# Scan stage of a six-layer kernel: parts of B and C made by ScalarE and TensorE, front products in two PSUM banks, decays in two

## What is computed

```
x_and_res = inputs @ W_in
x, res = jnp.split(x_and_res, 2, axis=-1)            # 256 channels each
x = jax.nn.silu(_depthwise_conv_same(x, K_conv, b_conv))   # 4 taps
x_dbl = inputs @ W_x                                  # 64 + 16 + 16 columns
delta, Bm, Cm = jnp.split(x_dbl, [DT_RANK, DT_RANK + D_STATE], axis=-1)
delta = jax.nn.softplus(delta @ W_dt + b_dt)
# for each channel and each of 16 states, over the 512 tokens:
#   h = exp(delta * A) * h + delta * x * Bm ;  y += h * Cm
y = y + x * D
y = y * jax.nn.silu(res)
return y @ W_out + b_out
```

## Time and profile before

| | us |
|---|---|
| median of three runs | 1669.47 (1667.58 to 1669.6) |
| the profiled execution, its own time | 1665.65 |
| its span | 1663.5 |
| first scan of the stage starts (in the span) | 787.7 |
| last scan of the stage starts | 1290.2 |
| busy over the whole span: TensorE, VectorE, GpSimd, ScalarE | 1404.0, 1172.5, 533.9, 513.2 |

### The profile page before, as it was taken

How to read it: one execution, slowest core, us unless ns; L and a number is a source line. 1 busy time by engine, 2 the same in 40 slices (tenths; PEclk the granted TensorE clock), 3 DMA queues, 4 the chain that set the end, 5 groups by cost and what they waited for, 6 DMA issues and landing times.

```text
span 1663.5 us, 21345 instructions
## 1 busy us (share of the span) xinstructions
PE 1404.0 (84%) x7226; PEld 1033.1 (62%) x7226; DVE 1172.5 (70%) x2629; ACT 513.2 (31%) x999; POOL 533.9 (32%) x447
## 2 busy tenths in 40 slices
PE   2887886595999999976888878878878599999998
PEld 2884545595899999952333333333323489999996
DVE  3786763585577776532998899999999557777753
ACT  2203444200222222223545445455353022222221
POOL 1150000001000000002788788888899100000000
PEclk9998997797899999986998989989998799999998
DMA  5550000553333333301332222323222233333330
GB/s 154 205 185 1 1 0 1 203 206 102 103 103 103 103 103 103 102 1 46 84 101 79 78 91 78 98 70 93 93 96 73 98 108 109 109 109 109 109 109 13
DMA packets 93162, 155.11 MB, mean 93 GB/s; under 512 B 11703, under 2 KB 21374, under 8 KB 92926
## 3 DMA queue, kind: packets, MB, share of 16 engines
q1 hardware_dynamic: 93054, 153.76, 28.5%
HBM read 150.31 MB, written 3.41 MB: 92 GB/s over the span
## 4 chain that ended last, share of the span: by engine, by line
PE 68%; DVE 16%; issue 8%; POOL 3%; ACT 2%; DMA 2%; DVEq 0%; POOLq 0%; SPq 0%; ACTq 0%
PE bank L1080 21%; PE bank L1198 7%; PE bank L1083 7%; PE bank L942 5%; PE bank L1142 3%; PE bank L973 2%; PE bank L1040 2%; DVE xe L1557 2%; DVE hs L1557 2%; DVE both L1549 2%; PE bank L1025 2%; POOL both L598 2%; PE bank L1092 2%; PE bank L1022 2%; PE bank L982 2%
## 5 line engine op out<-in xcount | busy, mean ns | idle before, releaser
L1080 PE MATMUL bank<-wqkv_sb,xe 128*128 128x192 f32 x2048 | 370.5, 334 | 10.0 <-DVE xe L1493 9.8
L1080 PEld LDWEIGHTS bank<-wqkv_sb,xe 128*128 128x128 f32 x2048 | 340.1, 194 | 21.4 <-DVE xe L1493 15.0
L1198 PE MATMUL bank<-both,ident 128*128 128x512 f32 x512 | 267.4, 650 | 17.3 <-DVE both L1549 16.4
L566 POOL TENSOR_TENSOR rstd<-ve,half_neg 128x4 f32<-128x4 f32 x32 | 37.6, 1173 | 734.0 <-DVE ve L1251 734.0
L843 ACT ACTIVATE bank<-dt,A 128x512 f32<-128x512 f32 x256 | 172.7, 685 | 169.6 <-DVE xe L1557 92.8
L1198 PEld LDWEIGHTS bank<-both,ident 128*128 128x128 f32 x512 | 105.0, 212 | 151.2 <-issue 108.3
L598 POOL TENSOR_TENSOR both<-du,prob 128x512 f32<-128x512 f32 x128 | 161.1, 1271 | 36.0 <-DVE xe L1557 19.8
L598 POOL TENSOR_TENSOR both<-du,prT 128x512 f32<-128x512 f32 x128 | 160.8, 1271 | 17.0 <-DVE hs L1557 12.5
L1557 DVE TENSOR_TENSOR_SCAN hs<-bank,both 128x512 f32<-128x512 f32 x128 | 153.7, 1212 | 0.0
L1557 DVE TENSOR_TENSOR_SCAN xe<-bank,both 128x512 f32<-128x512 f32 x128 | 152.8, 1210 | 0.3 <-issue 0.3
L942 PE MATMUL bank<-exp_sb,xe 128*128 128x128 f32 x1024 | 128.1, 283 | 27.1 <-DVE xe L1376 26.5
(11 more groups left out here) (261 smaller groups left out, 2011.4 us busy)
## 6 DMA issues: line engine op xcount, KB each, us to landing
dt<-w_rows SPq DMA_DIRECT2D x128, 256.0 KB, 4.2
du<-w_rows SPq DMA_DIRECT2D x128, 256.0 KB, 5.2
prob<-bc_dram SPq DMA_DIRECT2D x64, 256.0 KB, 3.3
prT<-bc_dram SPq DMA_DIRECT2D x64, 256.0 KB, 3.3
dt<-g_dram SPq DMA_DIRECT2D x32, 256.0 KB, 5.6
du<-g_dram SPq DMA_DIRECT2D x32, 256.0 KB, 6.7
g<-g_dram SPq DMA_DIRECT2D x32, 256.0 KB, 6.5
u<-g_dram SPq DMA_DIRECT2D x32, 256.0 KB, 6.4
```

The lines of the kernel that those rows point to most:

```text
L566: pool.tensor_tensor(rstd[:], ve[:], half_neg[:, 0:NT], ALU.pow).then_inc(ln_rstd, 1)
L1080: m = pe.matmul(bank[4 + j // 2][:, (j % 2) * 3 * HD:(j % 2 + 1) * 3 * HD], x_e, wqkv_sb[:, e, :], start=(e == 0 and j % 2 == 0), stop=(e ...
L1198: pe.matmul(bank[4 + k % NH][:], ident[:], hc[k % HRING], start=False, stop=(SUM_RANK[k] == sums_of(k // UNITS, k % NH))).then_inc(hc_used, 1)
```

## The change

It does six things in the scan stage.

- **Parts of B and C.** The steps `rows` and `bcT`, VectorE's copy and the five split operations go. ScalarE copies B and C from the dlt product twice, once as bf16 (the first part, into `bcT3`) and once as float32 (`bc_rows`, there before too). TensorE then makes, in float32, bc_rows minus the parts so far (one product with the identity, one with `less`, which holds -1), and ScalarE copies the result as the next bf16 part; this happens twice.
- **Banks.** Front products lie in two banks: conv0, conv1, z0, res0 in bank 2; xT, dlt and the two rests, z1, res1, out in bank 7. Each waits for the one before it in its own bank.
- **Decays.** Bank 2 was one of three decay banks, so two remain. ScalarE now makes the decay of scan U+1 in slot U, and it waits for the scan two before.
- **Slots.** All tables of front steps are new; `out` moves from slot 6 to 7, the addition to x from 8 to 10, the DMA of B and C to DRAM from slot 2 to slot 31.
- **Order within a front.** dlt stands between the two halves of conv0.
- **Waits.** th, lz and thr each have one buffer, and ScalarE now waits for VectorE's use of them, as bank 7 no longer orders it.

```
-FRONT7 = {"xT": -8, "rows": -6, "conv0": -4, "dlt": 0, "bcT": 2, "conv1": 8, "z0": 12, "z1": 16, "res0": 20, "res1": 22}
-OUT7 = 6
+FRONT7 = {"xT": -7, "dlt": -4, "conv0": -3, "conv1": 5, "z0": 11, "z1": 12, "res0": 17, "res1": 20}
+OUT7 = 7
+FRONT_IN = {"xT": 7, "dlt": 7, "conv0": 2, "conv1": 2, "z0": 2, "z1": 7, "res0": 2, "res1": 7, "out": 7}
...
-        decay = [bank[0], bank[6], bank[2]]
+        decay = [bank[0], bank[6]]
+        front_bank = {name: bank[i] for name, i in FRONT_IN.items()}
...
+                    if b >= 2:
+                        act.wait_ge(C_ps, seen(states_on_dve(NS * (b - 1))))
+                    act.activation(bcT3[par][0:32, :], front_bank["dlt"][DR:W3, :], ACT.Copy).then_inc(bcT_sb, 1)
+                    act.activation(dlt[0:DR, :], front_bank["dlt"][0:DR, :], ACT.Copy).then_inc(dlt_sb, 1)
                     if b:
                         act.wait_ge(bc_out, 16 * b)
-                    act.activation(bc_rows, bank[7][DR:W3, :], ACT.Copy).then_inc(dlt_sb, 1)
-                    yield
-                    act.wait_ge(bank7_ps, seen(IN7["bcT", b]))
-                    act.activation(bcT3[par][:], bank[7][0:W3, 0:L // 2].bitcast(BF16), ACT.Copy).then_inc(bcT_sb, 1)
-                    yield
+                    act.activation(bc_rows, front_bank["dlt"][DR:W3, :], ACT.Copy).then_inc(dlt_sb, 1)
+                    yield
+                    tanh_u(0)
+                    yield
+                    for part in (1, 2):
+                        act.wait_ge(part_ps, seen(2 * b + part))
+                        act.activation(bcT3[par][32 * part:32 * (part + 1), :], front_bank["dlt"][0:32, :], ACT.Copy).then_inc(bcT_sb, 1)
+                        yield
...
-                steps = on_clock(front, (-10, -7, -1, 1, 3, 11, 13, 14, 17, 18, 21, 23))
+                steps = on_clock(front, (-10, -6, -3, -1, 1, 3, 7, 12, 13, 15, 16, 18, 22))
                 for U in SCAN_CLOCK:
-                    if 0 <= U + 2 < ALL:
-                        decay_of(U + 2)
+                    if 0 <= U + 1 < ALL:
+                        decay_of(U + 1)
                     due(steps, U)
...
+                    for part in range(2):
+                        pe.wait_ge(dlt_sb, seen(2 * (b + 1)))
+                        pe.wait_ge(bcT_sb, seen(3 * b + part + 1))
+                        pe.matmul(front_bank["dlt"][0:32, :], ident[0:32, 0:32], bc_rows, start=True, stop=False)
+                        m = pe.matmul(front_bank["dlt"][0:32, :], less[0:32 * (part + 1), :], bcT3[par][0:32 * (part + 1), :], start=False, stop=True)
+                        m.then_inc(part_ps, 1)
+                        yield
...
-                steps = on_clock(front, (-8, -6, -4, -2, 0, 2, 8, 10, 12, 16, 20, 22), back, (OUT7,))
+                steps = on_clock(front, (-7, -5, -4, -3, -1, 2, 3, 5, 11, 12, 17, 20), back, (OUT7,))
...
-                steps = on_clock(front, (-13, -11, -5, 0, 12, 15, 19, 22, 24), back, (4, 5, 8))
+                steps = on_clock(front, (-13, -11, 1, 9, 15, 18, 20, 24), back, (4, 5, 10))
```

More of the change, by code:

```diff
@@ L160 @@
                + [(UNITS * (b + 1) + OUT7, "out", b) for b in range(NB)])
-BEFORE7 = {TURNS[i + 1][1:]: TURNS[i][1:] for i in range(len(TURNS) - 1)}
+BEFORE7 = {}
+for i in (2, 7):
+    there = [turn[1:] for turn in TURNS if FRONT_IN[turn[1]] == i]
+    BEFORE7.update(zip(there[1:], there))
 IN7 = {turn[1:]: i + 1 for i, turn in enumerate(t for t in TURNS if t[1] not in ("xT", "out"))}
@@ L1132, in front @@
                     pe.wait_ge(xT_sb, seen(g + 1))
[L1133 to L1137, removed]
                     def conv(h):
                         into_bank7(f"conv{h}", b)
-                        pe.matmul(bank[7][:], bias3[:, P + h * P:P + (h + 1) * P], ones3[:], start=True, stop=False)
+                        to = front_bank[f"conv{h}"][:]
+                        pe.matmul(to, bias3[:, P + h * P:P + (h + 1) * P], ones3[:], start=True, stop=False)
                         for tap in range(4):
-                            m = pe.matmul(bank[7][:], wcv[:, tap, h * P:(h + 1) * P], xpad[:, tap:tap + L], start=False, stop=(tap == 3))
+                            m = pe.matmul(to, wcv[:, tap, h * P:(h + 1) * P], xpad[:, tap:tap + L], start=False, stop=(tap == 3))
                             if tap == 1:
@@ L1146, in conv @@
                         yield
-                    yield from conv(0)
+                    conv0 = conv(0)
+                    pe.wait_ge(xT_sb, seen(g + 1))
+                    next(conv0)
+                    yield
                     into_bank7("dlt", b)
-                    pe.matmul(bank[7][0:W3, :], wx_sb[:], xpad[:, 1:L + 1], start=True, stop=True).then_inc(bank7_ps, 1)
+                    pe.matmul(front_bank["dlt"][0:W3, :], wx_sb[:], xpad[:, 1:L + 1], start=True, stop=True).then_inc(bank7_ps, 1)
                     yield
[L1152 to L1157, removed]
-                    yield
+                    next(conv0)
+                    yield
+                    for part in range(2):
[5 more added lines that the diff above has]
+                        yield
                     yield from conv(1)
@@ L1161, in front @@
                         into_bank7(f"z{h}", b)
-                        pe.matmul(bank[7][:], wdt_sb[:, h * P:(h + 1) * P], dlt[:], start=True, stop=True).then_inc(bank7_ps, 1)
+                        pe.matmul(front_bank[f"z{h}"][:], wdt_sb[:, h * P:(h + 1) * P], dlt[:], start=True, stop=True).then_inc(bank7_ps, 1)
                         yield
@@ L1170, in back @@
                     into_bank7("out", b)
-                    pe.matmul(bank[7][:], ones3[:, 0:P], bout3[:], start=True, stop=False)
+                    pe.matmul(front_bank["out"][:], ones3[:, 0:P], bout3[:], start=True, stop=False)
                     for h in range(NH):
@@ L1539, in back @@
                     dve.wait_ge(acc_ps, seen(NB + b + 1))
-                    dve.tensor_tensor(seq(b), seq(b), bank[7][:], ALU.add).then_inc(acc_used, 1)
+                    dve.tensor_tensor(seq(b), seq(b), front_bank["out"][:], ALU.add).then_inc(acc_used, 1)
                     yield
```

64 lines of the change are left out of this document (27 added, 37 removed).

## The result

The changed kernel takes 1652.71 us (median of six runs, 1648.43 to 1655.66) against 1668.82 for the kernel before; the ratio is 0.9904, with a 95% interval from 0.9886 to 0.9922. It is 16 us faster. The forecast was 1629: right in its direction, and 24 us too good.

A forecast was written before the change was run, and what follows sets the result against it. VectorE's queue was taken as the bound. From 1665.65 us profiled, 30.7 in the scans (53.3 removed less 22.6 new stalls) and 9.7 in the lead-in gave 1625.2, so a 1629 median; range 1614 to 1640 (0.55).

The forecast's parts named there:

- VectorE's work: Scan stage: VectorE's work after the change is 57.2 us a cycle, the floor, above GpSimd's 55.4.
- The waits that go: VectorE's waits in the scans: 14.7 for tanh, 6.5 "issue", 4.1 for C, 3.3 for the output product disappear.
- The split: Removed split operations and copy on VectorE, third scan to last: 24.7 us saved, 4.1 a cycle.
- Lead-in: Before the first scans, the front chain gets shorter: scan 2 comes 9.7 us earlier, bounds 6 to 12.
- Slot 12: ScalarE's table load and az waiting for z0 make scan 14 2.4 us late, first element 1.2; 15.6 in all.
- Slot 9: Product waits for its C row on TensorE: 0.4 us, seven times, 2.8 in all.
- Slot 29, the three copies: Three ScalarE copies and dlt's arrival each make scan 31 0.35 us late; 0.7, six times, 4.2.
- Rival 1: TensorE's clock falls to half around slot 25, costing 3.0 to 4.3 us six times: 1647 to 1655; chance 0.20.
- Rival 3: Slower: with two decays, ScalarE's waits for TensorE stop scans; 10 us more a cycle gives 1689; chance 0.05.
- Rival 2: No new stalls in the scans: cycle falls to its floor, up to 22.6 us less, 1606; chance 0.12.
- Rival 4: GpSimd becomes the bound: two microseconds lost at its du steps, cycle 63, time 1643; chance 0.04.
- Rival 5: No change: removed time returns as waits for the same tiles at other slots, 1668 to 1673; chance 0.04.

The follow-up runs named there:

- the fillers: Changed kernel plus four half-width float32 products on TensorE in slots 24, 25 and 26, results overwritten unread; 1642.39 us, ratio 0.9842.
- third buffer: Changed kernel with three buffers in place of two for the parts of C (`bcT3`); 1636.68 us, ratio 0.9813.
- version with all edits: Changed kernel plus third buffer, the fillers, table load alone in slot 10, softplus from slot 14, dlt in slot 27, two copies in slot 28; 1612.94 us.

## Why the prediction was right and wrong

- **VectorE's work, 57.2 a cycle: right in size, in part by luck.** It is busy 57.28 in the changed kernel, and cycles are 57.9 once no scan waits for a decay. But the prediction took off 4.1 for the split, the mean of the cycles, where the cycle that it started from had 4.7, and the norm grew by 0.9: 60.98 less 4.7 plus 0.9 is 57.2.
- **The waits that go, 28.6 by four rows: nearly right.** In the stretch of scans 3.2 for a product are left, one in the first element and one in the last. A wait of 1.6 for the output product stands behind the last scan and doesn't count.
- **The split, 24.7: over-sized by about 5.** The operations are gone, but between scan 2 and the last scan VectorE's busy time fell by 19.7, from 461.1 to 441.4. Two operations of the norm, on 128x4 elements, take 4.5 longer in all (below, on VectorE and GpSimd), though the change left them as they were, and so did the prediction. In the kernel before, taking away four of five operations gave 12.2 in place of 18.7, because two of the casts left stood for 3.3 each.
- **Lead-in, 9.7: right,** 11.1.
- **Slot 12, 15.6: right in kind and nearly in size.** 1.10 + 6 x 1.95 = 12.8; az did wait for z0 (six times 0.86), a little less than the 1.35 counted.
- **Slot 9, 2.8: right.** It was 0.40, six times (2.4).
- **Slot 29, the three copies, 4.2: this step failed.** It measured 28.3. The prediction let the copies start when dlt lands. They also wait for the last row of C of the running element, a wait that the diff shows, and I priced it at nothing. And it took TensorE to be at full clock here. At full clock the lateness is 1.06 for copies and dlt (0.7 was counted) and 2.0 for the C row; that makes 3.06, measured once and reproduced by the fillers. The half clock adds 1.6 to 2.3 in each of the other five. The third buffer and the fillers show the two causes, each alone and both together.
- **Rival 1, the clock: it happened,** with 0.20 given to it, and at half its price, some 2 in place of 3.0 to 4.3 a cycle (with the third buffer, one cycle lost 3.2 by it). That the measured 1652.71 lies in its range of 1647 to 1655 is luck: about half of the loss is the C row, which this rival does not have. The fillers gave back 10 us with two buffers (1652.71 to 1642.39) and 5 with three (1636.68 to 1631.26).
- **Rival 3: its mechanism, at half its size.** It said that every wait of ScalarE for TensorE stops the scans, and asked for 6.7 more in each cycle than counted. The copies of slot 29 are such a wait, and the three stalls cost 3.5 more a cycle than counted (43.5 less 22.6, over six).
- **Rivals 2, 4 and 5 did not occur.** Rival 2's time, 1606, is nearly reached by the version with all edits, which took the stalls away one by one.

The sum: 53.3 less 22.6 was forecast for the stretch of scans. With the stalls as measured it is 53.3 less 43.5 (12.8, 2.4 and 28.3), or 9.8. The 3.2 of waits that did not go and the 4.5 of the norm take that to 2.1. Small waits of the kernel before that the prediction did not count and that went too, 2.2 (1.5 of them for g), less a new one of 0.5, make it 3.8, against the 4.5 by which the stretch got shorter. So the miss is in the main the 24.1 by which slot 29 cost more than counted.

## What to carry to other kernels

When a step moves into an earlier phase, list every wait it issues, buffer reuse above all, and ask where the instruction that frees the buffer stands now; a double buffer by parity is not double when the writer runs two elements ahead. In an in-order queue with a short ring behind it, price the latest of all arrivals, not the data's alone. And when small operations are lengthened by what a neighbouring engine does, their busy time is not theirs alone: take some away, and others can take up part of it.

## What the runs showed of the hardware

**TensorE's clock follows idle time in pieces.** In the changed kernel it fell to 0.50 within slots 24 to 28 in five cycles of six; where the rows above show it, this came after a stretch in which TensorE stood idle between short groups (busy 1.74 and 1.02 of 2.50). With fillers of about 1.7 us a cycle it was at 1.00 from slot 26 to slot 30 in all six, while it still fell in slots 21 to 25 in some, and the time was 10 us shorter. The rule of the Trainium skill that the prediction named (TensorE: Matmul & The Clock Gate, section "A second HAM failure mode: psum-queue depth-cycling") tells of pauses between groups in a bf16 kernel that goes through PSUM banks. The trace, of a float32 kernel, agrees as to the swing and the loss. The fillers filled pauses and left the kernel's own products in their banks and order, and the swing left the critical stretch. So here it was enough to fill the pauses; whether the way through the banks plays a part no run tests, as the fillers themselves are groups in bank 2.

**A small operation of VectorE can stand still for a whole one of GpSimd.** Two equal subtractions of 128x128 in one cycle of the kernel before:

```profile
1106.63 1.25 DVE L1277 TENSOR_TENSOR bc_r<-bc_f,bc 128x128 f32<-128x128 f32 x1
...
1109.13 0.29 DVE L1279 TENSOR_TENSOR bc_r<-bc_r,bc 128x128 f32<-128x128 f32 x1
```

And GpSimd at that time:

```profile
1106.47 2.54 POOL L598 TENSOR_TENSOR both<-du,prob 128x512 f32<-128x512 f32 x2
1110.96 1.27 POOL L598 TENSOR_TENSOR both<-du,prob 128x512 f32<-128x512 f32 x1 [1.95 <-DVE xe L1557]
```

The first took 1.25, beside two operations of GpSimd of 1.27 each; the second took 0.29, with GpSimd idle from 1109.01 to 1110.96. By the Trainium skill (SBUF — State Buffer, section "SBUF: two separate sides") GpSimd shares one pair of ports with those operations of VectorE that have two SBUF inputs or run in a two-port mode. The pair is an exclusive lock: who starts first has it for its whole instruction, and the other is blocked. The trace agrees for these subtractions, which have two SBUF inputs. The cast left alone has one; which mode it runs in no run shows. Its 3.31 end within 0.1 of the end of the third of three GpSimd operations in a row.

So the time of such an operation depends on where GpSimd stands. The split went, and two operations of the norm got longer, which the prediction did not expect. First before, then in the changed kernel:

```profile
L1503 DVE SCALAR_TENSOR_TENSOR nmr<-mv,rstd 128x4 f32<-128x4 f32 x6 | 2.5, 408 | 0.0
L1245 DVE TENSOR_TENSOR mv<-stats 128x4 f32<-128x4 f32 x6 | 1.0, 166 | 0.2
...
L1511 DVE SCALAR_TENSOR_TENSOR nmr<-mv,rstd 128x4 f32<-128x4 f32 x6 | 5.4, 893 | 0.0
L1253 DVE TENSOR_TENSOR mv<-stats 128x4 f32<-128x4 f32 x6 | 2.6, 433 | 0.2
```

In the changed kernel each of these twelve stands beside a GpSimd operation and ends within 0.1 of that one's end. They take 4.5 us more than before.
